# Who makes the one-hot rows of the destinations while a graph's edges are counted: VectorE in one comparison, or ScalarE in two activations

## What is computed

```python
def _sparse_attention(x, src, dst, wq, bq, wk, bk, wv, bv, wo, bo):
    ...
    scores = jnp.einsum('ehd,ehd->eh', q[src], k[dst])
    smax = jax.ops.segment_max(scores, src, num_segments=N)
    ex = jnp.exp(scores - smax[src])
    denom = jax.ops.segment_sum(ex, src, num_segments=N)
    attn = ex / denom[src]
    out = jax.ops.segment_sum(attn[:, :, None] * v[dst], src, num_segments=N)

def _gcn_conv(x, src, dst, W, b, n):
    h = x @ W
    deg = jax.ops.segment_sum(jnp.ones_like(dst, dtype=x.dtype), dst, num_segments=n)
    dis = jnp.where(deg > 0, jax.lax.rsqrt(jnp.maximum(deg, 1.0)), 0.0)
    msg = h[src] * (dis[src] * dis[dst])[:, None]
    return jax.ops.segment_sum(msg, dst, num_segments=n) + b
```

## Time and profile before

| | us |
|---|---|
| median of 3 runs | 2005.14 (2004.68 to 2005.87) |
| the profiled execution, its own time | 2002.6 |
| its span, first to last instruction | 2000.8 |
| PE busy over the span | 1916.7 (96%) |
| DVE busy | 1368.3 (68%) |
| ACT busy | 789.4 (39%) |
| POOL busy | 458.3 (23%) |

### The profile page before, as it was taken

One profiled execution on the slowest core, in us unless ns is written; L12 is line 12 of the kernel. 1 busy time (PEld: TensorE's weight loads), 2 busy tenths in 40 slices (PEclk: granted clock), 3 DMA queues, 4 the chain that ended last, 5 costly groups with the idle time before them and its releaser, 6 DMA issues. The chain is left out here.

```text
span 2000.8 us, 33572 instructions
## 1 busy us (share of the span) xinstructions
PE 1916.7 (96%) x11664; PEld 1571.6 (79%) x11664; DVE 1368.3 (68%) x2830; ACT 789.4 (39%) x1527; POOL 458.3 (23%) x521
## 2 busy tenths in 40 slices
PE   6989999999999999999999999999999999899999
PEld 3446878988889888888998898889988888765543
DVE  7887668888865588878647888885488787640111
ACT  1332455555432355554224555542255554330000
POOL 1000333121332421304324112152231122500000
PEclk9999999999999999999999999999999999999999
DMA  4113462111200112011102110301121106120001
GB/s 134 43 46 73 134 191 60 36 48 37 91 32 32 51 49 58 25 48 68 43 22 80 42 36 25 115 1 42 47 61 36 35 25 167 29 51 1 0 21 31
DMA packets 50719, 108.36 MB, mean 54 GB/s; under 512 B 18143, under 2 KB 18195, under 8 KB 50608
## 3 DMA queue, kind: packets, MB, share of 16 engines
q1 hardware_dynamic: 50608, 106.87, 18.2%
HBM read 83.60 MB, written 23.25 MB: 53 GB/s over the span
## 5 line engine op out<-in xcount | busy, mean ns | idle before, releaser
L1490 PE MATMUL ps<-kT,qg 128*125 128x512 f32 (+1 forms) x1440 | 313.6, 362 | 14.2 <-DVE nmx L1143 11.5
L1490 PE MATMUL ps<-PT,V 125*128 125x250 f32 x2400 | 312.9, 284 | 1.7 <-DVE PT L1159 1.7
L1143 DVE CUSTOM_DVE_ANT_0 pbuf<-ps,bt 125x1250 f32<-125x1250 f32 x160 | 233.3, 1458 | 115.3 <-PE ps L1583 105.9
L1490 PEld LDWEIGHTS ps<-kT,qg 128*125 128x125 f32 x1440 | 246.0, 187 | 81.7 <-issue 18.9
L776 ACT ACTIVATE PT<-ps 125x500 fp32r<-125x500 f32 (+1 forms) x480 | 214.6, 520 | 237.9 <-PE ps L1583 237.9
L1490 PEld LDWEIGHTS ps<-PT,V 125*128 125x128 f32 x2400 | 289.6, 190 | 2.9 <-DVE PT L1159 2.9
L770 ACT ACTIVATE pbuf<-pbuf,nmx 125x1250 f32<-125x1250 f32 x160 | 215.0, 1344 | 165.3 <-DVE nmx L1143 165.3
L1159 DVE TENSOR_TENSOR PT<-ps,PT 125x500 fp32r<-125x500 f32 (+1 forms) x480 | 253.4, 584 | 2.5 <-ACT PT L776 2.2
L1583 PE MATMUL ps<-ident,pbuf 125*125 125x125 f32 x1600 | 205.5, 276 | 13.2 <-DVE pbuf L1152 13.2
L1583 PEld LDWEIGHTS ps<-ident,pbuf 125*125 125x125 f32 x1600 | 190.1, 191 | 16.1 <-DVE pbuf L1152 15.5
L508 POOL CAST qg<-qc 128x250 fp32r<-128x250 f32 x80 | 46.2, 578 | 475.5 <-PE ps L1490 436.8
(11 more groups left out here) (189 smaller groups left out, 2647.9 us busy)
## 6 DMA issues: line engine op xcount, KB each, us to landing
bt<-edge_bias_scratch SPq DMA_DIRECT2D x40, 546.9 KB
q_scratch<-qc SPq DMA_DIRECT2D x16, 500.0 KB, 2.6
qc<-q_scratch SPq DMA_DIRECT2D x16, 500.0 KB, 4.6
counts_scratch<-cblk SPq DMA_DIRECT2D x10, 546.9 KB
c_rows<-counts_scratch SPq DMA_DIRECT2D x10, 546.9 KB
edge_bias_scratch<-b_rows SPq DMA_DIRECT2D x10, 546.9 KB
counts<-counts_scratch SPq DMA_DIRECT2D x10, 546.9 KB
wm<-in_L_gnn_wo_dram SPq DMA_DIRECT2D x4, 1024.0 KB, 8.2
```

What stands on the lines that cost most here:

```text
L1143: v.tensor_tensor_reduce(out=P[:, u, :], in0=ps_S, in1=bt[:, u, :], scale=-1.0, scalar=FLOOR, op0=ALU.add, op1=ALU.min, accum_out=nmx[:, u ...
L1490: e = mm(out_, lhs(a), rhs(b), start=start and i == 0, stop=stop and i == 2)
```

## The change

The rows of `oh_dst` move from DVE to ACT. For a destination d and an edge with destination e the row needs 1 where d = e and 0 elsewhere. ACT has no comparison; it computes |d - e| in one activation (`away`, with the bias -e from `edgeT`, whose destinations are now stored negated) and relu(1 - |d - e|) in a second, with the bias from a column of ones (`unity`). DVE keeps `oh_src`.

PE waits for two semaphores a chunk instead of one. ACT makes the first trio of tile t+1 (`dst_first`) right behind tile t's last trio, ahead of the copy of tile t, and the remaining trios (`dst_rest`) behind that tile's copy and its other work of that place. The sine embedding moves behind the first tile's copy. One subtraction of the conditioning (`cond_low`) moves on DVE from ahead of tile 8 to ahead of tile 9. POOL sets one more constant.

```diff
+        away = early("away", [T, 2, TRIO, T], F16)
...
+            def dst_trio(t, chunk0, used):
+                ring = t % 2
+                for b in range(TRIO):
+                    act.wait_ge(s[f"dsthot{ring}"], used + (b + 1))
+                    settled(act)
+                    sc.activation(away[:, ring, b, :], iota16[:, t * T:(t + 1) * T], ACT.Abs,
+                                  bias=edgeT[:, 1, bass.ds(chunk0 + b, 1)]).then_inc(s[f"away{ring}"], 1)
+                for b in range(TRIO):
+                    act.wait_ge(s[f"away{ring}"], used + (b + 1))
+                    act.wait_ge(s[f"oh_used{ring}"], used + (b + 1))
+                    settled(act)
+                    sc.activation(oh_dst[:, ring * TRIO + b, 0:T], away[:, ring, b, :], ACT.Relu, bias=unity[:, :],
+                                  scale=-1.0).then_inc(s[f"dsthot{ring}"], 1)
+            def dst_first(t):
+                first = act.value_load(tab[0:1, t:t + 1], min_val=0, max_val=ECP - TRIO)
+                before = 0 if t < 2 else act.value_load(tab[0:1, 2 * NT + t:2 * NT + t + 1], ...)
+                trios = act.value_load(tab[0:1, NT + t:NT + t + 1], min_val=1, max_val=EC // TRIO + 1)
+                dst_trio(t, first, act.snap(before * TRIO) if t >= 2 else 0)
+                return first, before, trios
+            def dst_rest(t, first, before, trios):
+                with act.Fori(1, trios) as i:
+                    used = act.snap((before + i) * TRIO)
+                    chunk0 = act.snap((first + i * TRIO).with_bounds(min_val=0, max_val=ECP - TRIO))
+                    dst_trio(t, chunk0, used)
...
+            act.wait_ge(s["tabi"], 1)
...
+            dst_rest(0, *dst_first(0))
+            following = dst_first(1)
             count_out(0)
+            embedding()
+            act.wait_ge(s["consts"], CONSTS)
             for t in range(1, NT):
...
+                dst_rest(t, *following)
+                if t + 1 < NT:
+                    following = dst_first(t + 1)
                 count_out(t)
                 blocks_out(t - 1)
...
-            v.tensor_copy(edgeT[:, :, 0:EC], ps[0:T, 7, 0:2 * EC].rearrange("p (a e) -> p a e", a=2)).then_inc(s["edgeT"], 1)
+            v.tensor_copy(edgeT[:, 0, 0:EC], ps[0:T, 7, 0:EC])
+            v.tensor_scalar(edgeT[:, 1, 0:EC], ps[0:T, 7, EC:2 * EC], -1.0, None, ALU.mult).then_inc(s["edgeT"], 1)
...
-                        v.tensor_scalar(oh_dst[:, slot, 0:T], iota16[:, t * T:(t + 1) * T],
-                                        edgeT[:, 1, bass.ds(chunk0 + b, 1)], None, ALU.is_equal)
...
                 if t == 9:
+                    cond_low()
                     front_norm(0, PROJECTED[0])
...
                         pe.wait_ge(s[f"onehot{ring}"], done + (q + 1))
+                        pe.wait_ge(s[f"dsthot{ring}"], done + (TRIO + q + 1))
```

More of the change, by code:

```diff
@@ L129, in build @@
         big = sb("big", [T, 1])
+        unity = sb("unity", [T, 1])
         stats = sb("stats", [T, 2, 6])
@@ L233, in build @@
         ps_q = ps[:, 6:8, :]
-        CONSTS = 16
-        EARLY_CONSTS = 8
+        CONSTS = 17
+        EARLY_CONSTS = 9
         s = {}
         for name in ("x_ld edge_ld small_ld brow_ld ident consts edge_f edge_t edgeT brow_t cols emb_u emb_r emb_f emb emb_h "
-                     "h1 cond_mm condT rm rel cand cand_t red red_t tab prefix tabi onehot0 onehot1 oh_used0 oh_used1 ct_mm ct ct_t ct_e "
+                     "h1 cond_mm condT rm rel cand cand_t red red_t tab prefix tabi onehot0 onehot1 dsthot0 dsthot1 away0 away1 oh_used0 oh_used1 ct_mm ct ct_t ct_e "
                      "i_st c_ld0 c_ld1 bln bmask bdone bst_out0 bst_out1 cnt_out0 cnt_out1 condS0 condS lnhi lnS onesr "
@@ L457, in _ @@
             pool.wait_ge(s["consts"], 7)
+            g.memset(unity[:, :], 1.0).then_inc(s["consts"], 1)
+            pool.wait_ge(s["consts"], 8)
             g.memset(edgeT[:, :, EC:ECP], -1.0).then_inc(s["consts"], 1)
-            pool.wait_ge(s["consts"], 8)
+            pool.wait_ge(s["consts"], 9)
             g.memset(zeros16[:, :], 0.0).then_inc(s["consts"], 1)
-            pool.wait_ge(s["consts"], 9)
+            pool.wait_ge(s["consts"], 10)
             g.memset(eps[:, :], EPS).then_inc(s["consts"], 1)
-            pool.wait_ge(s["consts"], 10)
+            pool.wait_ge(s["consts"], 11)
             g.memset(ln_at[:, :], LN_AT).then_inc(s["consts"], 1)
-            pool.wait_ge(s["consts"], 11)
+            pool.wait_ge(s["consts"], 12)
             g.memset(big[:, :], BIG).then_inc(s["consts"], 1)
-            pool.wait_ge(s["consts"], 12)
+            pool.wait_ge(s["consts"], 13)
             g.memset(condT[:, :], 1.0).then_inc(s["consts"], 1)
-            pool.wait_ge(s["consts"], 13)
+            pool.wait_ge(s["consts"], 14)
             g.memset(lnw[:, :, :], 0.0).then_inc(s["consts"], 1)
-            pool.wait_ge(s["consts"], 14)
+            pool.wait_ge(s["consts"], 15)
             g.memset(condS[:, :].bitcast(F32), 0.0).then_inc(s["consts"], 1)
-            pool.wait_ge(s["consts"], 15)
+            pool.wait_ge(s["consts"], 16)
             g.memset(lnS[:, :, :].bitcast(F32), 0.0).then_inc(s["consts"], 1)
@@ L619, in _, with embedding @@
             sc = nc.scalar
-            act.wait_ge(s["emb_f"], 1)
-            sc.activation(embT[:, :], phr[:, :], ACT.Sin, scale=6.2831850).then_inc(s["emb"], 1)
-            act.wait_ge(s["consts"], CONSTS)
+            def embedding():
+                act.wait_ge(s["emb_f"], 1)
+                sc.activation(embT[:, :], phr[:, :], ACT.Sin, scale=6.2831850).then_inc(s["emb"], 1)
+            def dst_trio(t, chunk0, used):
[13 more added lines that the diff above has]
+                first = act.value_load(tab[0:1, t:t + 1], min_val=0, max_val=ECP - TRIO)
+                before = 0 if t < 2 else act.value_load(tab[0:1, 2 * NT + t:2 * NT + t + 1], min_val=0, max_val=(EC // TRIO + 1) * NT)
+                trios = act.value_load(tab[0:1, NT + t:NT + t + 1], min_val=1, max_val=EC // TRIO + 1)
[6 more added lines that the diff above has]
+                    dst_trio(t, chunk0, used)
             def h1_out(i):
@@ L687, in rsqrt0 @@
                 sc.activation(r0[:, :], lnv[:, :], ACT.Exp, scale=-0.5).then_inc(s["r0"], 1)
+            act.wait_ge(s["tabi"], 1)
+            act.wait_ge(s["edgeT"], 1)
+            act.wait_ge(s["prefix"], 3)
+            act.wait_ge(s["consts"], EARLY_CONSTS)
+            dst_rest(0, *dst_first(0))
+            following = dst_first(1)
             count_out(0)
+            embedding()
+            act.wait_ge(s["consts"], CONSTS)
             for t in range(1, NT):
@@ L1045, in cond_split, with cond_low @@
                 v.tensor_copy(condS[32:32 + C + 1, :], condT[:, :]).then_inc(s["condS0"], 1)
+            def cond_low():
                 dve.wait_ge(s["condS0"], 1)
```

1 line of the change is left out of this document (added).

## The result

| | us |
|---|---|
| changed kernel, median of 4 runs | 2044.61 (2041.32 to 2045.96) |
| kernel before, 4 runs beside them | 2005.51 (2004.68 to 2008.57) |
| ratio, 95% interval | 1.019 (1.0172 to 1.0207) |
| span of the profiled execution | 2039.5, against 2000.8 |
| start of the stage's last copy | 214.18, against 177.5 |

The changed kernel is slower by 1.9%. Of the span's 38.7 us, 36.7 lie in the counting stage.

What follows compares the result with a forecast made beforehand. VectorE was taken to pace counting at 0.617 us a chunk; ScalarE would match that pace with its other work now in the path: +23 us over the tiles, +4.4 for clock, total +27, giving 2032 us, range 2012 to 2050.

Steps and rivals of the forecast that it cites:

- ScalarE becomes the pace: Counting loop: ScalarE's six activations take 1.85 us a trio, 0.617 a chunk, just VectorE's present pace.
- its other work enters the path: Tiles 2 to 7: ScalarE's formerly free work lengthens periods, by +4.7 us in tile 3 and +8.75 in tile 6.
- the sum: Counting stage: the shifts of all tiles' periods add to +23 us, before the clock.
- VectorE's saving: Counting loop: VectorE loses 186 comparisons, worth -12 us if nothing else paced; with ScalarE's pace it wins nothing.
- Tiles 0 and 1: Stage's start: ScalarE's later start and table loads put tile 1's copy at 53.4 against 48.89, +4.5 us.
- Register reads: Between tiles: ScalarE's register reads for the next tile's dst_first take 1.5 us, ahead of the copy.
- The clock: TensorE's idleness in tiles 3 and 6 brings two slow stretches at 2.2 us each, +4.4 us.
- rival A: Slower still: ScalarE's sequencer paces a trio at 2.2 us, or the clock falls more often; +21 more, 2053; chance 0.15.
- A's second cause: TensorE's new idle of about 2 us at each tile's end lowers the clock more often.
- Tile 9: Nothing to make ahead and cond_low hides in VectorE's spare time: 13.4 us against some 13.8, -0.4.
- tile 8: With cond_low moved behind it, tile 8 takes 19.25 us against 23.17, -3.9.
- Behind the stage: After the counting stage: TensorE work untouched by the change, so the stage's shift reaches the kernel's end whole.

Runs made afterwards that it cites:

- run without z: Changed kernel without ScalarE's ten activations on z in tile 6: 2035.54 us, ratio 1.0154 to the kernel before.
- run with zeros: Changed kernel with matmuls of zeros on TensorE where it idles, adding nothing to the counts: 2033.15 us, ratio 1.0152 to the kernel before.
- run of the order alone: Kernel before, VectorE making both one-hots, with the sine embedding behind the first copy and cond_low ahead of tile 9: 2006.7 us, ratio 1.0021.
- three mends: Changed kernel with registers read a tile earlier (ratio 1.0137), matmuls of zeros on TensorE (1.0152) or cond_low back ahead of tile 8 (1.0181); together 1.0102.
- run with `cond_low` back at 8: Changed kernel with the subtraction cond_low back ahead of tile 8: 2040.62 us, ratio 1.0181 to the kernel before.
- after: The changed kernel itself, with the whole change and no further edit: 2044.61 us, ratio 1.019 to the kernel before.
- before: The kernel without the change, VectorE making both one-hot matrices: 2005.51 us.

## Why the prediction was right, and where its sizes were off

**ScalarE becomes the pace, and its other work enters the path: right.** The trio was put at 1.85 us and measured 1.905. The prediction's estimate by the formula of the Trainium skill (ScalarE: Activation LUTs, What ACT_TABLE_LOAD costs), 1.75, left out the 0.05 for loop and registers that its own 1.85 has; with it the trio is 1.80, and the sum 3 us smaller, not 6. The run without z and the run with zeros show the mechanism tile by tile: 7.1 us for 7.14 of work, and periods of 16.61, 21.31, 18.70, 16.81, 24.94 and 15.76 where the sum has 16.85, 21.25, 18.7, 16.85, 25.0 and 15.5. VectorE's saving bought nothing, as forecast; it waits 65.2 us for slots.

**Tiles 0 and 1: right.** The copy of tile 1 was put at 53.4 and started at 53.69. In the run of the order alone tile 1's copy came 1.4 us later, too little for the whole time to show.

**Register reads: right in place and size** (1.5 forecast, 1.3 to 2.0 in the timeline at the ends of tiles 1 to 8). Of the three mends tried alone, reading them early gained most.

**The clock: the term that was mis-sized.** The prediction gave two low stretches, 4.4 us. There were some 48 us at the low level instead of 13, and those that zeros could remove cost 10.0 us in tiles 3 to 9. The step that failed is the one that set rival A aside: "the idleness at a tile's end is shorter than the 3.40 that is known to have preceded a slow tile". TensorE's waits of 2.0 to 2.5 us at a tile's end also stood right ahead of low stretches, in tiles 3, 4, 7 and 8, though not in 2, 5 or 6, which had waits of 2.0 to 2.1. In the run with `cond_low` back at 8 they stood ahead of one in tiles 2 and 5 and of none in tile 7, so which wait it is differs by execution. A's second cause was thus real, at 5.6 us where A in all had 21, while its first (a trio of 2.2) was wrong. That the time of 2044.61 lies between the forecast and A comes from this and from tile 9, not from the pace.

**Tile 9: the step that failed.** "cond_low there hides: VectorE has 3 us a tile to spare", -0.4. It measured 18.94 against 13.4. VectorE had the time for the 1.45 us: without the 2.9 us by which the norm is stretched, the comparison at 199.87 below would have started at 196.9, and TensorE was free at 197.5. What was not priced is POOL's work that waits for `cond_low` and came down on the norm. VectorE's timeline of after ahead of tile 9, and POOL's:

```profile
193.75 0.98 DVE L1134 TENSOR_TENSOR nt_b<-nt_a,r 125x2 f32<-125x2 f32 x1
...
194.97 2.29 DVE L1138 TENSOR_TENSOR rstd<-nt_c,r 125x2 f32<-125x2 f32 x1
...
199.87 1.46 DVE L1027 TENSOR_SCALAR oh_src<-iota,edgeT 125x1250 bf16<-125x1250 f16 x3 [1.50 <-issue]
```
```profile
194.90 2.34 POOL L491 TENSOR_TENSOR lnS<-lnw,lnS 17x1024 fp32r<-17x1024 f32 x1 [0.19 <-POOL lnS L487]
```
TensorE then sat 3.02 us ahead of 200.55, and the clock was low from 198.8. In the run with `cond_low` back at 8, tile 9 takes 13.70.

**The sum closes.** Forecast last copy 204.6 (53.4 + 16.85 + 129.95 for tiles 3 to 9 + 4.4), measured 214.18. The 9.6 us between are: clock 10.0 - 4.4 = 5.6; tile 9 with zeros 18.28 - 13.4 = 4.9, of which about 1.5 is again the clock, behind the long wait; tile 8 with zeros 18.05 - 19.25 = -1.2; all other tiles together +0.3. The clock's 10.0 holds as far as zeros change nothing but the clock. They also stand in TensorE's queue, and they leave tile 9's low stretch, so the clock cost after at least that.

**Behind the stage: as forecast, but for 2 us.** 1825.3 us against 1823.3, with TensorE busy 1766.65 and 1766.09. Over after and its edits it lay between 1820.9 and 1825.3 with no pattern, over before and its edits between 1820.3 and 1823.6, and no run aimed at it: open.

Open too: why some waits of about 2 us at a tile's end leave the clock alone and others don't. Two further ways weren't tried: more slots in the rings, so that ScalarE could make more than one trio ahead, and POOL as the maker of `oh_dst`.

## What to carry to other kernels

Before work goes to an idle engine, list what that engine does inside the loop now: with only one trio ahead, that work, and the register reads too, moved onto the path here at full length. When an operation is moved, follow whoever waits for it: what `cond_low` cost in the changed kernel was not its 1.45 us but the 2.9 us by which POOL's two operations behind it stretched the norm. And where TensorE gets new gaps, a gap shorter than any that the trace shows ahead of a low stretch is not thereby free: bound it by the price of the seen ones.

## What the runs showed of the hardware that was not expected

- A VectorE operation on two numbers a partition lasted 2.28 and 2.29 us beside a POOL subtraction of 2.33 and 2.34 us, against 0.16 alone. A comparison with one tensor input was held as well, 2.33 us against 0.26, beside one of 2.51.
- Waits of TensorE of 2.0 to 2.5 us, with dense matmuls between them, stood ahead of stretches at the 1.2 GHz level in four tiles of seven; with matmuls of zeros in these and the longer waits the stage's clock went from 0.88 to 0.98. A wait of the same 2.04 us in the same tile 2 was followed by nine matmuls in 1.81 us in one execution, and by eighteen in 4.86 in another.
- Three register reads cost ScalarE 1.3 to 2.0 us of idle time, and 0.19 to 0.25 where they stood behind a tile's copy.
